# Centred input in pieces, second half one step later, and another order at the start

## Chip, core and metric

The kernel runs on one core of one Trainium2 chip. The metric is the device time of one execution in microseconds. Engines: TensorE (PE), VectorE (DVE), ScalarE (ACT), GpSimd (POOL) and SyncE (SP), which issues the transfers.

## What is computed

`x` is 4 sequences of 1024 tokens with 128 features. Four layers, each on a layer norm of x and added to it:

```
x = x + attn_a(ln(x))    # inside: conv of 4 taps, q/k/v with running means, a small gelu FFN
x = x + ffn(ln(x))       # sum over 8 experts: (silu(x Wg) * (x Wu)) Wd, 128 -> 512 -> 128
x = x + attn_b(ln(x))    # 16 heads of 8, ALiBi, causal
x = x + ffn(ln(x))       # the same experts again
```

`attn_a` on one sequence h = ln(ln(x)): `x1 = ln(x) + conv(h)`, then `q, k, v` of ln(x1); `pq = cumsum(q) / position`, `pk = cumsum(pq * k) / position`, `x2 = x1 + pk * v`, and `x2 + Wu gelu(Wb ln(x2))`. Only the first layer (the "sequence work") and the first FFN are touched here.

## The kernel before

**Tiles.** A sequence is 8 blocks of 128 tokens (`BLK`), in two halves of 512 (u = 0, 1). The FFN goes over 8 tiles of 512 tokens; a tile has 32 chunks of 128 hidden features. x lies in SBUF all the time.

**The first FFN with the sequences beside it.** `ffn(f)` runs pairs of tiles (= one sequence). In a pair there are 64 steps p, one per chunk. In step p TensorE does the sequence stages of p, then gate and up of chunk p + 2 (L1118 to L1120, twice three products), then down of chunk p (L1125 to L1127). ScalarE does silu of chunk p + 1 (L1639), the rounded part `h_hi` of chunk p (L1657), then its sequence stages. VectorE does the product of chunk p + 1 (L2093), the rest `h_lo` of chunk p (L2114), then its stages. The down product of p waits for `h_hi` and `h_lo` of p. Each engine takes its stream in order. The first pair is written out ("first"), the next two are a loop ("middle"), the last has no sequence beside it. Pair i has sequence i + 1 beside it.

**The order of the sequence work** is a table by hand, `AT`: for each stage the step for half 0 and for half 1. `at(p, kind)` asks whether a stage is due at p: in the first pair ten steps later than the table (`SHIFT_FIRST`), in the middle pairs three later (`TAPS_LATER`) for all but `tok`, `T1` and `copy`. Stages in the order of data: `tok` centres the input by blocks, four per half, on VectorE (`a0_tok`, L1926) and on ScalarE (`hc_tok`, L1542); `T1` transposes both; `copy` takes them from PSUM; `conv` (L879 in the middle pairs, from `taps`, which SyncE writes to memory and loads back shifted, L583 and L586); `a1` (L1935) adds; `T5`, `stats5` (L1903, L1907), `norm5` (L1553), `T7`, `h2`; `q`, `cumq`, `k`, `kq`, `cumk`, `v`, `vq`; `T9`, `stats9`, `norm9` (L1553), `T10`, `h3` (L1560); `up` (L943; four products; for half 1 all in one step, with the four copies `hid1` on VectorE, L1988, one step earlier in the table); `gelu` (L1573, all four parts at once, with a load of ScalarE's gelu table before it and one of silu's after it); `down` (L952), `y` (L1992), `T13`, `x1` (L1996). GpSimd has the roots of the inner norms, the two means (L677, L680) and one addition (L684). The norm of the next tile stands at `NORM_AT`: in middle pairs statistics at step 10, norm (L1874) at 13, transposes at 14.

```
       "up": (32, 37), "gelu": (36, 41), "down": (42, 44), "y": (43, 45), "T13": (44, 46),
UP_AT = [AT["up"][0] + c for c in range(4)] + [AT["up"][1]] * 4
    return UP_AT[4] - 1 if name == "hid1" else AT[name][u]
```

So in a middle pair the gelu of half 0 is at step 39, the up products of half 1 at step 40 and the gelu of half 1 at step 44, with the down products of half 0 at step 45.

**The start.** Sequence 0 runs before the FFN, half 0 ahead; the order is written out by calls `first_step(stage, u)` in every engine. VectorE's `stats_of_input(lo, hi)` takes statistics of input blocks (L1894, L1897). GpSimd's `low_part(r, m)` (L689) splits a quarter of a weight; `norms_of_input` takes the roots for all blocks and waits for all statistics. Stages that half 1 of sequence 0 has left run in the first steps of the first pair (`LEFT`, `left(p)`).

Of the kernel before, what the change touches and what calls it, by code (L numbers as in the profile page):

```python
# [140 lines left out]
def rests_by_pool(p):  # L141
# [9 lines left out]

AT = {"tok": (0, 1), "T1": (2, 4), "copy": (2, 4), "conv": (5, 6), "a1": (6, 7), "T5": (7, 8),
# [11 lines left out]
SHIFT_FIRST = 10  # L166
NORM_AT = {"first": (12, 24), "middle": (10, 16), "last": (13, None)}
LOW_LATE = 13
LEFT = {"stats9": 0, "norm9": 2, "T10": 3, "h3": 3, "up": (4, 4, 5, 5), "hid1": (4, 4, 5, 5), "gelu": 6,
        "down": (8, 8, 9, 9), "y": 9, "T13": 10, "x1": 10}  # L170


def position(name, u, c=0):

    if name in ("up", "down"):
        return (UP_AT if name == "up" else DOWN_AT)[u * 4 + c]
    return UP_AT[4] - 1 if name == "hid1" else AT[name][u]


# [3 lines left out]
def at(p, kind):  # L183

    def now(name, u, c=0):
        later = 0
        if kind == "first":
            later = SHIFT_FIRST
        elif name not in AHEAD_OF_TAPS:
            later = TAPS_LATER  # L190
        return position(name, u, c) + later == p
    return now

# [19 lines left out]
def only(*wanted):  # L213
    return lambda *stage: stage == wanted
# [14 lines left out]
def build(nc, ap):  # L229
    x_in, out = ap["hidden"], ap["out"]  # L230
    with ExitStack() as ctx:
# [366 lines left out]
        def _(pool):  # L598
# [105 lines left out]
            pool.wait_ge(s["a_n5"], BLK)  # L704
            low_part(1, 1)
            low_part(1, 2)
            low_part(2, 0)
            low_part(2, 1)
            pool.wait_ge(s["rinv_ready"], 5)
            sequence_step(0, only("cumq", 1), True)  # L710
            sequence_step(0, only("cumk", 1), True)

            def rstd4(f, n0, mv=mv, lnw=lnw):
# [41 lines left out]
            def ffn_beside_sequences(f):  # L755

                def norm(t):
                    pool.wait_ge(f["mv"], t * SUB + SUB)
                    rstd4(f, t * 2)

                def pair(i, kind):
                    for p in range(2 * CH):
                        if kind == "first" and p == LOW_LATE:
                            pool.wait_ge(s["a_tokd"], 2 * BLK)
                            for m in range(3):
                                low_part(3, m)
                        sequence_step(i + 1, at(p, kind))
                        if p % CH == NORM_AT[kind][p // CH]:
                            norm(i * 2 + (p // CH + 1))

                norm(0)
                pool.wait_ge(f["norm"], SUB)
                low_part(2, 2)
                sequence_step(0, left(0), True)
                norms_of_input(BLK, B * BLK)
                pair(0, "first")
                with pool.Fori(1, TILES // 2 - 1) as i:
                    pair(i, "middle")
                for p in range(2 * CH):
                    if p == NORM_AT["last"][0]:  # L780
                        norm(TILES - 1)
                    if p >= PROJECT_FROM and (p - PROJECT_FROM) % PROJECT_STEPS == 2:
                        root_of_projected((p - PROJECT_FROM) // PROJECT_STEPS)
                    if p in REST_BY_POOL:
                        pool.wait_ge(f["hhi"], LAST_PAIR + p + 1)
                        g.tensor_tensor(h_lo[:, p % 2, :], hid[:, p % 4, :], h_hi[:, p % 2, :].bitcast(F32),
                                        ALU.subtract).then_inc(f["hlo_pool"], 1)
                    if p >= PROJECT_FROM:
                        project_step(*divmod(p - PROJECT_FROM, PROJECT_STEPS))
                    if p == SPLIT_EARLY:  # L790
                        split_max(0)
                third_part(LAST - 1, 1)
# [52 lines left out]
        def _(pe):  # L845
# [115 lines left out]
            def first_step(*stage):  # L961
                sequence_step(0, only(*stage), True)
# [40 lines left out]
            first_step("T5", 1)  # L1003
            first_step("T10", 0)
            first_step("T7", 1)
            for c in range(4):
                first_step("up", 0, c)
            first_step("q", 1)
            first_step("k", 1)
            for c in range(4):  # L1010
                first_step("down", 0, c)
# [482 lines left out]
        def _(act):  # L1494
# [32 lines left out]
            def sequence_step(b, now, first=False):  # L1527

                for u in range(2):
                    ahead = first and u == 0  # L1530
                    src, sl = bank(0 if ahead else 5 + u), slice(u * NT, (u + 1) * NT)
                    blocks = range(SUB * u, SUB * (u + 1))
                    if now("tok", u):

                        if first:
                            act.wait_ge(s["a_lnx"], 9 * (u + 1))
                        else:
                            act.wait_ge(s["a_lns"], b)
                            act.wait_ge(s["a_dn"], b * 2)
                        ln = lnx if first else lns  # L1540
                        for j in blocks:
                            a.activation(hc_tok[:, j * P:(j + 1) * P], xs(b * BLK + j), ACT.Identity,  # L1542
                                         bias=ln[:, L_BOTH_BIAS, j:j + 1],
                                         scale=ln[:, L_BOTH, j:j + 1]).then_inc(s["a_toka"], 1)
# [31 lines left out]
            def first_step(*stage):  # L1576
                sequence_step(0, only(*stage), True)
# [4 lines left out]
                for m in range(3):  # L1582
                    a.copy(w_hi[m][:, quarter], w_raw[m][:, quarter]).then_inc(s[f"split_hi{r}"], 1)

            first_step("tok", 0)
            conv_matrices()
            act.wait_ge(s["par_ready"], 1)
            first_step("copy", 0)
            high_part(0)
            first_step("tok", 1)  # L1590
            other_matrices()
            first_step("copy", 1)
            first_step("h2", 0)
# [242 lines left out]
        def _(dve):  # L1836
# [71 lines left out]

            def sequence_step(b, now, first=False):

                if now("tok", 0) and not first:

                    v.tensor_copy(lns[:], lnx[:, :, bass.ds(b * BLK, BLK)]).then_inc(s["a_lns"], 1)
                    dve.wait_ge(s["a_lns"], b)
                for u in range(2):
# [1 line left out]
                    src, other = (bank(0), bank(1)) if ahead else (bank(5 + u), bank(6 - u))  # L1917
                    sl = slice(u * NT, (u + 1) * NT)
                    blocks = range(SUB * u, SUB * (u + 1))
                    if now("tok", u):  # L1920
                        if first:
                            dve.wait_ge(s["a_lnx"], 9 * u + 2)
                        for j in blocks:
                            mean = mvx[:, j, 0:1] if first else lns[:, L_MEAN, j:j + 1]
                            rstd = (lnx if first else lns)[:, L_RSTD, j:j + 1]
                            v.tensor_scalar(a0_tok[:, j * P:(j + 1) * P], xs(b * BLK + j), mean, rstd,  # L1926
# [77 lines left out]
                stats_of_input(u * SUB, u * SUB + SUB)  # L2004
            positions()
            quarter_of_positions(0)
            first_step("tok", 0)
            quarter_of_positions(1)
            parameters()
            first_step("copy", 0)  # L2010
            first_step("tok", 1)
            quarter_of_positions(2)
            dve.wait_ge(s["par_ready"], 1)
            first_step("a1", 0)
# [16 lines left out]
            projections()  # L2031
            v.memset(x[:, 0:NT], 0.0)
            dve.wait_ge(s["x_rest_loaded"], 16 * (B - 1))
            stats_of_input(BLK, 2 * BLK + SUB)
            first_step("cumq", 1)
            first_step("kq", 1)
            first_step("cumk", 1)
            first_step("y", 0)
# [50 lines left out]
            def ffn(f):  # L2089
# [9 lines left out]
                def pair(i, kind):  # L2099
                    last = kind == "last"  # L2100
                    for h in range(2):
                        t = i * 2 + h
                        end = last and h == 1
                        for c in range(CH):
# [18 lines left out]
                                continue  # L2123
                            if kind == "first":
                                sequence_step(0, left(h * CH + c), True)
                            if kind == "first" and h * CH + c == SHIFT_FIRST:
                                dve.wait_ge(s["a_lnx"], 28)
                            if not last:
# [12 lines left out]
                                project_step(*divmod(c - PROJECT_FROM, PROJECT_STEPS))  # L2141

                first_norm(f, 5)
                stats_of_input(2 * BLK + SUB, B * BLK)
                dve.wait_ge(f["up"], 1)
                dve.wait_ge(f["silu"], 1)
                product(0)
# [276 lines left out]
```

## Time and profile before

| | us |
|---|---|
| median of 3 runs | 1780.88 (1780.56 to 1783.27) |
| profiled execution | 1783.65 |
| its span, first to last instruction | 1781.9 |
| mean granted TensorE clock | 0.986 |
| first FFN, first to last gate/up product | about 61 to 765 |

In a row of the timeline stand: start in us from the span's start, length in us, engine, line, operation, output <- inputs, shapes, count of merged instructions, and in brackets the engine's idle time just before and what ended it. A product of 512 columns follows the one before it after 0.23 us at the full clock.

### The profile page before, as it was taken

Reading aid. Unit: us, or ns where it says so; the run is one execution under the profiler, and the core shown is the slowest. Engines: PE = TensorE matmul, PEld = TensorE weight load, DVE = VectorE, ACT = ScalarE, POOL = GpSimd, SP = SyncE. Lnnn points to the kernel's source line nnn. Section 1 sums busy time; section 2 is a strip of 40 time slices with the busy share of each in tenths; the row PEclk is TensorE's granted clock in tenths of the full one; section 3 lists DMA queues with packets and bytes.
Section 4 is the critical chain, followed back from the end, with each engine's and each line's share of the span. In section 5 each row is a group of like instructions: output and inputs, shape, how many; then the busy total and the mean of one; then the engine's idle time right before and its main releaser. Section 6 shows DMA issues by size and latency. Waiting matters only on the chain.

```text
span 1781.9 us, 28475 instructions
## 1 busy us (share of the span) xinstructions
PE 1694.8 (95%) x10265; PEld 1098.4 (62%) x10265; DVE 1256.3 (71%) x2133; ACT 1039.4 (58%) x1690; POOL 478.2 (27%) x648
## 2 busy tenths in 40 slices
PE   5799999999999999988889999999999999999998
PEld 3567677777767877633335555555555555558876
DVE  7677577766766777777777777777777777646665
ACT  6445755555565555466656666566666566665554
POOL 6522001100210123421114444334444443440000
PEclk8899999999999999989999999999999999999999
DMA  6000011002000122223010100000000000010000
GB/s 213 0 1 1 1 30 31 1 1 59 4 0 0 41 88 84 84 78 101 28 46 2 36 24 20 7 24 25 14 24 24 18 8 2 2 31 1 6 7 6
DMA packets 63423, 52.35 MB, mean 29 GB/s; under 512 B 7983, under 2 KB 58558, under 8 KB 63294
## 3 DMA queue, kind: packets, MB, share of 16 engines
q1 hardware_dynamic: 63120, 50.57, 9.7%
q8 instruction: 79, 1.29, 0.3%
q14 instruction: 50, 0.41, 0.1%
q10 hardware_dynamic: 174, 0.07, 0.0%
HBM read 32.40 MB, written 18.22 MB: 28 GB/s over the span
## 4 chain that ended last, share of the span: by engine, by line
PE 81%; DVE 7%; ACT 5%; issue 3%; DMA 1%; POOL 1%; SPq 0%; ACTq 0%; DVEq 0%
PE ps L1263 8%; PE ps L1226 7%; PE ps L1264 6%; PE ps L1265 6%; PE ps L1118 5%; PE ps L1120 5%; PE ps L1119 5%; PE ps L1091 4%; PE ps L1295 4%; PE ps L1060 3%; PE ps L849 3%; PE ps L1297 3%; PE ps L1296 3%; PE ps L1125 3%; PE ps L1127 3%
## 5 line engine op out<-in xcount | busy, mean ns | idle before, releaser
L1633 ACT ACTIVATE pr<-ps 128x1024 f32<-128x1024 f32 (+2 forms) x285 | 267.8, 945 | 188.7 <-PE ps L1048 115.5
L2093 DVE TENSOR_TENSOR hid<-sg,ps 128x512 f32<-128x512 f32 x256 | 174.8, 683 | 192.2 <-PE ps L1120 142.4
L809 POOL TENSOR_TENSOR h_lo<-hid,h_hi 128x512 fp32r<-128x512 f32 x176 | 225.6, 1282 | 265.2 <-ACT h_hi L1733 260.7
L1639 ACT ACTIVATE sg<-ps 128x512 f32<-128x512 f32 x256 | 153.7, 600 | 238.1 <-PE ps L1120 235.7
L2083 DVE TENSOR_REDUCE negp<-ps 128x2 f32<-128x1024 f32 (+2 forms) x224 | 254.6, 1145 | 51.0 <-PE ps L1048 30.4
L1118 PE MATMUL ps<-xn_hi,w_hi 128*128 128x512 f32 x512 | 227.3, 444 | 0.6 <-DVE xn_lo L1889 0.6
L1263 PE MATMUL ps<-xn_hi,w_hi 128*128 128x512 f32 x512 | 223.5, 437 | 0.7 <-DVE hid L2220 0.6
L2220 DVE SCALAR_TENSOR_TENSOR hid<-sg,ps 128x512 f32<-128x512 f32 x176 | 121.0, 687 | 126.4 <-ACT sg L1723 125.7
L1264 PE MATMUL ps<-xn_lo,w_hi 128*128 128x512 f32 x512 | 202.2, 395 | 0.0
L1120 PE MATMUL ps<-xn_hi,w_lo 128*128 128x512 f32 x512 | 202.1, 395 | 0.0
L1119 PE MATMUL ps<-xn_lo,w_hi 128*128 128x512 f32 x512 | 202.0, 394 | 0.0
L1265 PE MATMUL ps<-xn_hi,w_lo 128*128 128x512 f32 x512 | 201.4, 393 | 0.0
L2114 DVE TENSOR_TENSOR h_lo<-hid,h_hi 128x512 fp32r<-128x512 f32 x236 | 176.0, 746 | 0.0
L1733 ACT CAST h_hi<-hid 128x512 fp32r<-128x512 f32 x256 | 157.5, 615 | 14.6 <-PE ps L1297 10.2
L1657 ACT CAST h_hi<-hid 128x512 fp32r<-128x512 f32 x256 | 157.6, 616 | 0.6 <-DVE hid L2093 0.4
L1723 ACT ACTIVATE sg<-ps 128x512 f32<-128x512 f32 x176 | 105.4, 599 | 77.3 <-PE ps L1265 76.0
L1226 PE MATMUL ps<-pr,vp 128*9 128x512 f32 (+3 forms) x1376 | 146.2, 498 | 0.0
L1091 PEld LDWEIGHTS ps<-qs,ks 63*128 63x128 bf16 x720 | 35.1, 93 | 168.0 <-issue 141.5
L1091 PE MATMUL ps<-qs,ks 63*128 63x512 bf16 (+2 forms) x720 | 114.5, 335 | 13.8 <-DVE negp L2083 9.7
L2226 DVE TENSOR_TENSOR hid<-hid,ps 128x512 f32<-128x512 f32 x176 | 120.3, 684 | 7.1 <-PE ps L1265 3.1
L1263 PEld LDWEIGHTS ps<-xn_hi,w_hi 128*128 128x128 f32 x512 | 95.9, 187 | 40.4 <-issue 18.7
L1060 PE MATMUL ps<-ks,qs 60*128 60x512 bf16 (+2 forms) x720 | 113.1, 330 | 6.2 <-DVE xn_lo L2210 2.6
(244 smaller groups left out, 3074.5 us busy)
## 6 DMA issues: line engine op xcount, KB each, us to landing
qs<-qd SPq DMA_DIRECT2D x60, 96.0 KB
ks<-kd SPq DMA_DIRECT2D x60, 96.0 KB
kd<-qkp SPq DMA_DIRECT2D x14, 256.0 KB, 2.9
qd<-qkp SPq DMA_DIRECT2D x7, 384.0 KB, 2.6
w_raw<-in_Wg SPq DMA_DIRECT2D x4, 512.0 KB, 7.4
w_raw<-in_Wu SPq DMA_DIRECT2D x4, 512.0 KB, 7.4
w_raw<-in_Wd SPq DMA_DIRECT2D x4, 512.0 KB, 8.7
work<-hd SPq DMA_DIRECT2D x8, 256.0 KB, 4.5
```

The costliest lines, as they stand in the source:

```text
L809: g.tensor_tensor(h_lo[:, q % 2, :], hid[:, q % 4, :], h_hi[:, q % 2, :].bitcast(F32), ALU.subtract).then_inc(FS[1]["hlo_pool"], 1)
L1091: mm = pe.matmul(dst[e], k_of(n)[r, hp, j * P:(j + 1) * P], q_of(n)[r, hp, from_q:from_q + w], start=True, stop=st not in MASKED)
L1118: pe.matmul(dst, w_hi[m][:, w], xn_hi[:, h, :], start=True, stop=False)
L1119: pe.matmul(dst, w_hi[m][:, w], xn_lo[:, h, :], start=False, stop=False)
L1120: pe.matmul(dst, w_lo[m][:, w], xn_hi[:, h, :], start=False, stop=True).then_inc(f[sig], 1)
L1226: mm = pe.matmul(ps[32 * h:32 * h + HD + 1, O_BANK, from_q:NT], vp[:, n % 2, j, h, :], pr_of(n, st)[:, h, 0:NT - from_q], start=(j == 0), ...
L1263: pe.matmul(dst, w_hi[m][:, w], xn_hi[:, h, :], start=True, stop=False)
L1264: pe.matmul(dst, w_hi[m][:, w], xn_lo[:, h, :], start=False, stop=False)
L1265: pe.matmul(dst, w_lo[m][:, w], xn_hi[:, h, :], start=False, stop=True).then_inc(f[sig], 1)
L1633: a.activation(pr_of(n, st)[:].rearrange("p (e a) q -> p e a q", e=2)[:, :, hps[0]:hps[-1] + 1, 0:WIDTH[st]], heads(buf, hps, WIDTH[st]), ...
L2083: v.tensor_reduce(to[:, :, hps[0]:hps[-1] + 1, i % SUB], heads(buf, hps, JOB_WIDTH[k]), AX.X, ALU.max, negate=True).then_inc(T["reduced"], 1)
L2114: v.tensor_tensor(h_lo[:, c % 2, :], hid[:, c % 4, :], h_hi[:, c % 2, :].bitcast(F32), ALU.subtract).then_inc(f["hlo"], 1)
```

## The change

It centres the input of a sequence in two pieces per half, two blocks each, at table steps 0, 1 (half 0) and 2, 3 (half 1), on both engines. In the middle pairs every other stage of half 1 but `T1` and `copy` comes one step later. In the start, TensorE does `q` of half 1 after two of the four up products of half 0; VectorE takes only four blocks of statistics near there (behind `cumq`), twelve at the FFN's start, and eight in pieces of two in steps 0 to 3; GpSimd does `cumq` after the low parts of quarter 1, one low part between the two means, one before the stages left over and one behind the first of them.

```diff
-AT = {"tok": (0, 1), "T1": (2, 4), "copy": (2, 4), "conv": (5, 6), "a1": (6, 7), "T5": (7, 8),
+AT = {"T1": (2, 4), "copy": (2, 4), "conv": (5, 6), "a1": (6, 7), "T5": (7, 8),
+TOK_AT = ((0, 1), (2, 3))
+    if name == "tok":
+        return TOK_AT[u][c]
@@ at
         elif name not in AHEAD_OF_TAPS:
-            later = TAPS_LATER
+            later = TAPS_LATER + u
@@ GpSimd, start
             low_part(1, 2)
-            low_part(2, 0)
-            low_part(2, 1)
             pool.wait_ge(s["rinv_ready"], 5)
             sequence_step(0, only("cumq", 1), True)
+            low_part(2, 0)
             sequence_step(0, only("cumk", 1), True)
@@ GpSimd, before the first pair
                 pool.wait_ge(f["norm"], SUB)
+                low_part(2, 1)
+                sequence_step(0, left(0), True)
                 low_part(2, 2)
-                sequence_step(0, left(0), True)
                 norms_of_input(BLK, B * BLK)
@@ TensorE, start
-            for c in range(4):
-                first_step("up", 0, c)
+            first_step("up", 0, 0)
+            first_step("up", 0, 1)
             first_step("q", 1)
+            first_step("up", 0, 2)
+            first_step("up", 0, 3)
             first_step("k", 1)
@@ ScalarE and VectorE, sequence_step
-                    if now("tok", u):
+                    for c in range(2):
+                        if not now("tok", u, c):
+                            continue
...
-                        for j in blocks:
+                        for j in blocks[2 * c:2 * c + 2]:
@@ VectorE, start
-            stats_of_input(BLK, 2 * BLK + SUB)
+            dve.wait_ge(s["rinv_ready"], 5)
             first_step("cumq", 1)
+            stats_of_input(BLK, BLK + SUB)
             first_step("kq", 1)
@@ VectorE, pair
                                 sequence_step(0, left(h * CH + c), True)
+                            if kind == "first" and h == 0 and c < SUB:
+                                stats_of_input(3 * BLK + 2 * c, 3 * BLK + 2 * c + 2)
...
-                stats_of_input(2 * BLK + SUB, B * BLK)
+                stats_of_input(BLK + SUB, 3 * BLK)
```

## Rows read from the trace of the kernel before

**Rows 1.** The page, busy time and share of each engine.
```profile
PE 1694.8 (95%) x10265; PEld 1098.4 (62%) x10265; DVE 1256.3 (71%) x2133; ACT 1039.4 (58%) x1690; POOL 478.2 (27%) x648
```

**Rows 2.** Timeline of TensorE, two successive down products, second middle pair.
```profile
538.84 0.40 PE L1125 MATMUL ps<-h_hi,w_hi 128*128 128x512 f32 x1
...
540.91 0.40 PE L1125 MATMUL ps<-h_hi,w_hi 128*128 128x512 f32 x1
```

**Rows 3.** Timelines of the start, VectorE and TensorE; last a window, PEclk the third from its end.
```profile
42.04 2.35 DVE L1894 BATCH_NORM_STATS2 stx<-x 128x6 f32<-128x128 f32 x12
...
50.01 0.75 DVE L1961 SCALAR_TENSOR_TENSOR work<-ps,par,work 128x512 f32<-128x512 f32 x1 [2.91 <-POOL work L677]
...
52.00 0.73 DVE L1992 SCALAR_TENSOR_TENSOR a0T<-ps,par,a0T 128x512 f32<-128x512 f32 x1
...
46.48 3.60 PE L952 MATMUL ps<-gel_first,wt 128*128 128x512 f32 x8
...
60.00:65.00 5.00, 4.36 (x12) 3.18 (x11) 4.50 (x26) 2.09 (x3) 0.85 (x1) 0.50 0.00 0
```

**Rows 4.** Timelines of GpSimd and VectorE, first pair, step 14.
```profile
111.12 7.93 POOL L689 TENSOR_TENSOR w_lo<-w_raw,w_hi 128x1024 fp32r<-128x1024 f32 x3
...
111.46 2.60 DVE L2114 TENSOR_TENSOR h_lo<-hid,h_hi 128x512 fp32r<-128x512 f32 x1
```

**Rows 5.** Timelines of ScalarE and TensorE, second middle pair, steps 0 and 1.
```profile
423.31 1.65 ACT L1542 ACTIVATE work<-x,lns 128x128 f32 x4 [1.81 <-DVE lns L1913]
...
426.98 0.47 PE L1125 MATMUL ps<-h_hi,w_hi 128*128 128x512 f32 x1 [1.42 <-DVE h_lo L2114]
```

**Rows 6.** Timelines of TensorE and VectorE, second middle pair, steps 9 to 13.
```profile
446.80 0.64 PE L879 MATMUL ps<-taps,w_taps 128*32 128x512 f32 x4 [0.91 <-DMA taps<-hd]
...
450.70 0.74 DVE L1935 SCALAR_TENSOR_TENSOR a0T<-ps,par,a0T 128x512 f32<-128x512 f32 x1
...
456.12 0.88 DVE L1903 BATCH_NORM_STATS2 sta<-ps 128x6 f32<-128x128 f32 x4
...
458.51 1.11 DVE L1874 TENSOR_SCALAR ntok<-x,mv,lnw 128x128 f32 x4
```

**Rows 7.** Timelines of ScalarE and TensorE, second middle pair, steps 33 and 34.
```profile
510.00 1.54 ACT L1553 ACTIVATE work<-ps,lna 128x128 f32<-128x128 f32 x4
...
510.50 0.47 PE L1125 MATMUL ps<-h_hi,w_hi 128*128 128x512 f32 x1
...
513.57 0.47 PE L1125 MATMUL ps<-h_hi,w_hi 128*128 128x512 f32 x1
```

**Rows 8.** Timelines of ScalarE, TensorE and VectorE, second middle pair, steps 39 and 40.
```profile
526.48 1.28 ACT L1573 ACT_TABLE_LOAD   x1
...
529.70 1.28 ACT L1639 ACT_TABLE_LOAD   x1
531.00 0.60 ACT L1639 ACTIVATE sg<-ps 128x512 f32<-128x512 f32 x1
531.49 0.61 ACT L1657 CAST h_hi<-hid 128x512 fp32r<-128x512 f32 x1
...
528.63 3.85 PE L943 MATMUL ps<-h2T,wt 128*128 128x512 f32 x8
...
534.62 0.47 PE L1125 MATMUL ps<-h_hi,w_hi 128*128 128x512 f32 x1 [0.74 <-ACT h_hi L1657]
...
529.70 1.61 DVE L1988 TENSOR_SCALAR work<-ps,par 128x512 f32<-128x512 f32 x2 [2.35 <-PE ps L943]
...
533.79 0.69 DVE L2114 TENSOR_TENSOR h_lo<-hid,h_hi 128x512 fp32r<-128x512 f32 x1
```

**Rows 9.** TensorE, first pair, steps 7 and 8: timeline, and the windows' row behind the gap.
```profile
90.39 0.76 PE L1125 MATMUL ps<-h_hi,w_hi 128*128 128x512 f32 x1 [2.94 <-ACT h_hi L1657]
...
95.83 0.40 PE L1125 MATMUL ps<-h_hi,w_hi 128*128 128x512 f32 x1
...
90.22:93.63 3.41, 3.23 (x6) 1.94 (x7) 1.23 (x3) 0.14 (x1) 0.00 (x0) 0.50 0.02 5
```

More of the change, by code:

```diff
@@ L1583, in high_part @@
                     a.copy(w_hi[m][:, quarter], w_raw[m][:, quarter]).then_inc(s[f"split_hi{r}"], 1)
-            first_step("tok", 0)
+            for c in range(2):
+                first_step("tok", 0, c)
             conv_matrices()
@@ L1589, in _ @@
             high_part(0)
-            first_step("tok", 1)
+            for c in range(2):
+                first_step("tok", 1, c)
             other_matrices()
@@ L1909, in sequence_step @@
             def sequence_step(b, now, first=False):
-                if now("tok", 0) and not first:
+                if now("tok", 0, 0) and not first:
                     v.tensor_copy(lns[:], lnx[:, :, bass.ds(b * BLK, BLK)]).then_inc(s["a_lns"], 1)
@@ L1919, in sequence_step @@
                     blocks = range(SUB * u, SUB * (u + 1))
-                    if now("tok", u):
+                    for c in range(2):
+                        if not now("tok", u, c):
+                            continue
                         if first:
                             dve.wait_ge(s["a_lnx"], 9 * u + 2)
-                        for j in blocks:
+                        for j in blocks[2 * c:2 * c + 2]:
                             mean = mvx[:, j, 0:1] if first else lns[:, L_MEAN, j:j + 1]
@@ L2006, in _ @@
             quarter_of_positions(0)
-            first_step("tok", 0)
+            for c in range(2):
+                first_step("tok", 0, c)
             quarter_of_positions(1)
@@ L2010, in _ @@
             first_step("copy", 0)
-            first_step("tok", 1)
+            for c in range(2):
+                first_step("tok", 1, c)
             quarter_of_positions(2)
```

## The prediction

> **What bounds the kernel now.** I read the page first: TensorE is busy for 95% of the span [rows 1], and no other engine is near that. So a microsecond counts only where TensorE stands still or runs at its lower clock. Then I read TensorE's timeline in the first FFN (63 to 765 us), the only part the change touches besides the start. Its unit is the step: the interval between the starts of two successive down products. A step that carries nothing of the sequence work takes 2.07 us [rows 2]; four transposes add 0.43 and a sequence product of 512 columns 0.87. What an interval has beyond such a sum is a stall. In the middle pairs (two passes of the loop, steps 0 to 63 each, the same pattern in both) I find these, each the distance of two down products less their work: step 0, 1.36 and 1.68 us; the tap transfers before the second convolution, about 1.2; steps 12 to 14, 0.9 in all; steps 25 to 28, 1.2; steps 32 and 33, 0.9; the gelu of the first half, 1.14.
>
> **The start.** VectorE does twelve statistics blocks before the scan of q, GpSimd is in its low parts and multiplies the mean only behind them, and the product with k waits 2.91 us for that mean, until 50.01 [rows 3]. The residual at L1992 comes at 52.00, though its four down products ended at 50.08 [rows 3]. After the change, q comes two products earlier on TensorE, only four blocks stand beside it, and GpSimd is free after two low parts. The total of TensorE's work up to the down products is the same. So L1992 is released by them: 50.15, a gain of 1.85, carried by the transpose, the addition, the statistics and the norm to the first gate product.
>
> Part of it goes back. Four steps now each carry two blocks of statistics on VectorE, about 0.65 us (0.4 for the blocks at the rate of the twelve at 42.04 [rows 3], the rest for two aggregates and their wait). In step 1 VectorE is the late one, because it has just done the inner statistics: 0.65 us of stall. The last low part of quarter 2 also moves behind the inner statistics of GpSimd, beside `h_lo`. What that does stands in the trace: with low parts running from 111.12, an `h_lo` of usually 0.69 takes 2.60 [rows 4]. VectorE and GpSimd take turns; one pass of about 2.6 (7.93 over three) delays the `h_lo` of step 2 by about 0.9 more. The Trainium skill (GPSIMD Engine Reference, Key points) speaks of contention with VectorE instructions that have two SBUF inputs; that speaks against this move, and the trace agrees, 2.60 against 0.69. Together the give-back is 1.5. Against it, TensorE's first gate and up products run at the half clock (0.50 from 60 to 65, its lower level of 1.2 GHz [rows 3]). They start 1.85 us earlier; if the clock also rises earlier by more than that, some of the products at 0.43 become 0.23. I take **-1.2** for the start, between -0.3 (clock rises when it did) and -2.0 (it rises before the first product).
>
> **The input in pieces.** At step 0 ScalarE has four activations of 1.65 us in one step and then silu and cast; TensorE stands 1.42 us before the next down product [rows 5]. Half of the activations leave 0.8 us less in front of the silu. The other halves move to steps 1, 2 and 3, where ScalarE has 0.8 us left over in a step of 2.07. The copy of the per-block constants, for which they wait, stays. So **-0.85** per middle pass and **-0.45** in the first pair, where the low parts of quarter 3 wait for the last piece, start 0.3 us later and meet the `h_lo` that TensorE waits for.
>
> **Second half one step later, steps 8 to 14.** The second convolution sits 0.91 us waiting for its taps after a half-empty slot [rows 6]. One step later the taps have been in for over 1 us: -1.15. But now step 11 on VectorE holds first the inner statistics of half 0 (1.3) and then the addition a1 of half 1 (0.74 [rows 6]), on which TensorE's transposes wait at the start of step 12: stall 0.66. And step 13 holds the inner statistics of half 1 (1.3, from 456.12) and the norm of the next tile (1.11 [rows 6]) together, so the transposes of that tile wait 1.15 instead of 0.3. Worked through to step 14 it is **+0.2** per pass: what the taps give, VectorE takes. Its ends are -1.2 (VectorE catches up) and +1.0 (GpSimd's passes fall on it too).
>
> **Steps 22 to 30.** The scan of q moves behind the product with v in the same step and TensorE's v product waits 0.6; one of the stalls behind GpSimd's passes at steps 26 to 28 goes. **+0.2** per pass, from -0.5 to +1.0.
>
> **Steps 32 to 35.** ScalarE now does h3 of half 0 and then the norm of half 1 (1.54) in one step, and the step takes 3.07 [rows 7], 0.57 more than its work. Apart, neither is late: **-0.6** per pass.
>
> **The gelu of half 0, the largest term.** It stays at step 39, since it belongs to half 0: table load, 1.91 us, table load, 526.48 to 530.98, and ScalarE's silu and cast of step 40 come behind it, the cast ending at 532.10 [rows 8]. Today TensorE fills that time with the four up products of half 1, which stand at step 40: 528.63, 3.85 us long [rows 8]. They belong to half 1 and move to step 41. Step 40 then has only a gate/up pair: TensorE is through with it at 530.02 and waits for `h_lo` of step 40, which can start at 532.1 and takes 0.69 [rows 8], so the down product starts at 532.98. That is a **gap of 2.96 us**. Then come the up products, with VectorE's four copies (from 529.70 today) between them. Today the down product stands 4.92 behind the first of those copies (534.62 [rows 8]); tomorrow the first copy is at 534.75, so the down product of step 41 is at 539.67. Today it is at 536.77: **+2.9** per pass. The gelu of half 1 moves with its half to step 45, where the down products of half 0 still stand; ScalarE starts it about 2 us later than today's, is done at 548.0, and TensorE has work until 550.6. Zero.
>
> Here a rule competes with the trace. From the rows, the silu starts 0.02 us behind its table load of 1.28, and I used that. The Trainium skill (ScalarE: Activation LUTs, What ACT_TABLE_LOAD costs) gives 2.66 us for every switch of tables with its drain. By that the gap would be 2.8 us longer per pass and my sum 5.5 higher.
>
> **The clock.** The trace has one other gap of this length in this part: 2.94 us before 90.39, also behind a gelu. The granted clock is 0.50 (1.2 GHz) for the 3.4 us behind it, and the interval to 95.83 is 5.44 us instead of 3.80 [rows 9]: 1.64 lost. Each of the two new gaps can cost between 0 (the clock stays, as behind the 1.42 of [rows 5]) and 1.6. I take 1.5, since they are nearest to the gap of 2.94.
>
> **Sum.** Start -1.2, first pair -0.45, per middle pass -0.85 + 0.2 + 0.2 - 0.6 + 2.9 + 1.5 = 3.35, twice 6.7: **+5.05**. The profiled execution took 1783.65, so 1788.7 for such a one; it lies 2.8 above the median of the runs shown, so I forecast a median of 1785.9. A measurement here can tell about 0.2% (3.6 us) from nothing.
>
> **Rivals.**
> - *The gap is there, but the clock stays up, and the small terms fall on the good side* (start -1.6, steps 8 to 14 at 0): -1.6 - 0.45 + 2 x 1.65 = +1.25, 1782.1: no change. For it: behind the 1.42 us of [rows 5] the clock stayed at 1.00. Against: 2.94 did. 0.30.
> - *The gelu stays covered and nothing new is late* (the other side). Place: the down product of step 40. If TensorE has as much queued before it as today, the penalties of steps 12 to 14, 22 to 30 and 40 vanish: -1.2 - 0.45 - 2 x (0.85 + 1.15 + 0.6) = -6.85, 1774.0. It decides from where the penalties of a pass stay under 1.65 us together; I have nearly 6. Against it: ScalarE runs in order, and nothing of step 40 can pass the table loads. 0.13.
> - *The rule of the tables holds where TensorE waits for ScalarE*, a drain of 1.38 per load that only shows then: 1785.9 + 5.5 = 1791.4. Against: the cast behind the loads is timed. 0.05.
> - My forecast: 0.52.
>
> **The numbers.** Slower by over 0.2% has the forecast and the table rival, 0.57; within 0.2%, 0.30; faster, 0.13. The low end, 1777.5, has the lower bounds of the terms (start -2.0, steps 8 to 14 at -1.2, no clock) and leaves most of the covered case out; the high end, 1790.5, has the clock at 1.6 twice and both VectorE terms at their upper bounds.
>
> **What would show it.** Right: in both middle passes a TensorE gap of nearly 3 us before the down product of step 40, behind an ACT cast, and 0.50 of clock behind it; no wait for taps; the second norm at step 34 without a stall; the transposes of step 12 waiting for a1, those of step 14 for the norm; L1992 near 50.1; one `h_lo` over 1.5 us near 71. Wrong: no gap at step 40, or up products still in front of it; taps still awaited; a start that is not earlier at the first gate product.

## The result, and the profile after

The changed kernel takes 1794.57 us, the median of six runs; the kernel before, run beside it, takes 1782.08. The ratio is 1.0064, its 95% interval 1.0052 to 1.0075: 11.4 us slower, between 9.3 and 13.4 (the two medians lie 12.5 apart). The forecast was slower by 5.05, with 1790.5 as the high end. The sign was right; the size was not.

The profiled execution has a span of 1794.6 against 1781.9, 12.7 more. The starts of the down products cut the first FFN into pairs and steps, and that shows where the 12.7 us arise.

| us | before | after | change |
|---|---|---|---|
| start of the second pair, from the span's start | 253.07 | 253.79 | +0.71 |
| first middle pass, 64 steps | 170.16 | 175.39 | +5.23 |
| second middle pass | 169.71 | 174.53 | +4.82 |
| last pair | 171.30 | 171.26 | -0.04 |
| from the FFN's last down product to the end | 1017.68 | 1019.60 | +1.92 |

And within the middle passes, the first and the second of them. A step p is here the time from the start of its down product to that of the next one:

| steps | before | after | change | forecast |
|---|---|---|---|---|
| 0 to 3, the pieces | 11.95, 12.28 | 11.55, 11.88 | -0.40, -0.40 | -0.85 |
| 7 to 14 | 22.42, 22.65 | 22.86, 22.85 | +0.44, +0.20 | +0.2 |
| 20 to 29 | 25.61, 25.59 | 26.65, 26.68 | +1.04, +1.09 | +0.2 |
| 31 to 35 | 14.37, 14.38 | 13.82, 13.81 | -0.55, -0.57 | -0.6 |
| 39 and 40, the gelu, with the clock | 8.84, 8.83 | 13.41, 13.48 | +4.57, +4.65 | +4.4 |

**The gelu of the first half.** TensorE's timeline in the first middle pass, as in [rows 8]: the down product of step 40, the up products of half 1, the down product of step 41.

```profile
363.71 0.48 PE L1130 MATMUL ps<-h_hi,w_hi 128*128 128x512 f32 x1 [2.97 <-ACT h_hi L1665]
...
364.49 5.29 PE L946 MATMUL ps<-h2T,wt 128*128 128x512 f32 x8
...
371.91 0.47 PE L1130 MATMUL ps<-h_hi,w_hi 128*128 128x512 f32 x1 [0.75 <-ACT h_hi L1665]
```

ScalarE's timeline in the same place: the two table loads, the silu and the cast. VectorE's `h_lo` of step 40, the last line, starts behind the cast and ends at 363.56; the down product waits for both, and starts 0.15 us behind it. (Its row names the cast, which had ended at 362.67.)

```profile
357.05 1.28 ACT L1579 ACT_TABLE_LOAD   x1
358.34 1.92 ACT L1579 ACTIVATE work<-work 128x2048 f32<-128x2048 f32 x1
360.28 1.28 ACT L1647 ACT_TABLE_LOAD   x1
361.57 0.60 ACT L1647 ACTIVATE sg<-ps 128x512 f32<-128x512 f32 x1
362.06 0.61 ACT L1665 CAST h_hi<-hid 128x512 fp32r<-128x512 f32 x1
...
362.88 0.68 DVE L2127 TENSOR_TENSOR h_lo<-hid,h_hi 128x512 fp32r<-128x512 f32 x1
```

The gap is 2.97 us, and behind it the four up products (eight matmuls) take 5.29 us where they took 3.85 [rows 8]. Windows in the gap, right behind it, and further on (PEclk is the third column from the end):

```profile
361.50:365.00 3.50, 1.29 (x5) 0.95 (x6) 1.29 (x2) 2.17 (x5) 0.00 (x0) 1.00 0.00 0
365.08:368.49 3.41, 3.41 (x5) 1.13 (x5) 1.50 (x2) 0.00 (x0) 0.00 (x0) 0.50 0.00 0
368.60:372.00 3.40, 2.65 (x10) 1.45 (x9) 2.94 (x5) 1.22 (x2) 0.00 (x0) 1.00 0.00 0
```

The clock is at its lower level of 1.2 GHz for 3.41 us, as behind the gap of [rows 9]; the second pass shows the same (0.50 from 539.16 to 542.57).

**The start.** TensorE from the transposes of T7 to the transposes that wait for L2002 (L1992 in the kernel before):

```profile
39.87 1.12 PE L852 MATMUL ps<-ident,work 128*128 128x128 f32 x4 [0.25 <-DVE work L1953]
...
47.65 3.60 PE L955 MATMUL ps<-gel_first,wt 128*128 128x512 f32 x8
51.08 1.02 PE L920 MATMUL ps<-h2T,wt 128*128 128x512 f32 x2
52.23 0.66 PE L852 MATMUL ps<-ident,a0T 128*128 128x128 f32 x4
```

And the same stretch before, whose row of the down products is in [rows 3]:

```profile
39.31 1.12 PE L849 MATMUL ps<-ident,work 128*128 128x128 f32 x4 [0.25 <-DVE work L1943]
...
49.91 1.02 PE L917 MATMUL ps<-h2T,wt 128*128 128x512 f32 x2
52.78 0.66 PE L849 MATMUL ps<-ident,a0T 128*128 128x128 f32 x4 [1.85 <-DVE a0T L1992]
```

The wait of 1.85 us that was to go is gone: TensorE now works through. But the down products end at 51.25 (50.08 before [rows 3]), and the last transposes start at 52.23, only 0.55 earlier. The stretch begins 0.56 later (39.87 against 39.31), and its product with v comes 1.17 later (51.08 against 49.91), so 0.61 more was lost on the way. That is in the clock, as the windows of before and after show (PEclk 0.76 and 0.58): counted from the stretch's own start, about 3.1 us at half clock before and 4.3 after, which costs 0.6 us more. Why the stretch begins later stays open.

```profile
40.00:45.00 5.00, 5.00 (x12) 2.38 (x11) 4.91 (x26) 4.16 (x6) 5.00 (x3) 0.76 0.01 3
```

```profile
40.00:45.00 5.00, 5.00 (x10) 2.53 (x11) 2.62 (x5) 3.76 (x5) 4.62 (x2) 0.58 0.01 3
```

**The give-back.** VectorE's timeline at the end of the start, then the `h_lo` of step 2 of the first pair:

```profile
48.24 0.75 DVE L1971 SCALAR_TENSOR_TENSOR work<-ps,par,work 128x512 f32<-128x512 f32 x1 [0.34 <-POOL work L680]
49.03 2.50 DVE L1978 TENSOR_TENSOR_SCAN work<-work,zcol 128x512 f32<-128x512 f32 x1
...
70.99 2.20 DVE L2127 TENSOR_TENSOR h_lo<-hid,h_hi 128x512 fp32r<-128x512 f32 x1
```

GpSimd beside them, the low part between the two means and the one behind the stages left over:

```profile
48.10 2.34 POOL L692 TENSOR_TENSOR w_lo<-w_raw,w_hi 128x1024 fp32r<-128x1024 f32 x1
...
70.25 2.40 POOL L692 TENSOR_TENSOR w_lo<-w_raw,w_hi 128x1024 fp32r<-128x1024 f32 x1
```

The product with k, which waits for the mean of q, waits 0.34 where it waited 2.91 [rows 3]. The `h_lo` takes 2.20 us beside GpSimd's low part. TensorE's down products of steps 1 and 2 then wait 0.76 (at 69.97) and 1.04 us (at 73.34). Steps 0 and 1 take 3.09 and 3.37 us where they took 2.44 and 2.17: +1.85.

**Steps 7 to 14.** TensorE's convolution, the transposes of step 12 and those of step 14:

```profile
278.18 1.07 PE L882 MATMUL ps<-taps,w_taps 128*32 128x512 f32 x8
...
284.07 0.65 PE L852 MATMUL ps<-ident,a0T 128*128 128x128 f32 x4 [0.47 <-DVE a0T L1945]
...
289.71 0.66 PE L852 MATMUL ps<-ident,ntok 128*128 128x128 f32 x4 [0.82 <-DVE ntok L1882]
```

**Steps 22 to 30.** TensorE's product with v and two later down products:

```profile
316.40 1.12 PE L920 MATMUL ps<-h2T,wt 128*128 128x512 f32 x2 [0.46 <-DVE work L1961]
...
326.89 0.48 PE L1130 MATMUL ps<-h_hi,w_hi 128*128 128x512 f32 x1 [0.45 <-ACT h_hi L1665]
...
332.02 0.47 PE L1130 MATMUL ps<-h_hi,w_hi 128*128 128x512 f32 x1 [0.73 <-DVE h_lo L2127]
```

GpSimd and VectorE ahead of the last of them: the addition on GpSimd, and the `h_lo` beside it, which is twice as long as usual (0.68).

```profile
330.03 1.29 POOL L687 TENSOR_TENSOR a0T<-a0T,work 128x512 f32<-128x512 f32 x1 [0.93 <-DVE work L1987]
```

```profile
330.47 1.41 DVE L2127 TENSOR_TENSOR h_lo<-hid,h_hi 128x512 fp32r<-128x512 f32 x1
```

In the kernel before, the same addition stood 4 us earlier, beside another `h_lo`, and TensorE waited 0.36 us for that one (GpSimd, VectorE, TensorE):

```profile
326.15 1.29 POOL L684 TENSOR_TENSOR a0T<-a0T,work 128x512 f32<-128x512 f32 x1
...
326.49 1.50 DVE L2114 TENSOR_TENSOR h_lo<-hid,h_hi 128x512 fp32r<-128x512 f32 x1
...
328.13 0.47 PE L1125 MATMUL ps<-h_hi,w_hi 128*128 128x512 f32 x1 [0.36 <-DVE h_lo L2114]
```

### The profile page after: what moved, and what is told of

It is laid out like the page before. It is cut to its first block, busy times and chain, and to the rows that moved or that the text cites. A ratio compares the mean times of both kernels' runs of the same rounds, so it can differ in the third digit from the quotient of the medians.

```text
span 1794.6 us, 28482 instructions
## 1 busy us (share of the span) xinstructions
PE 1700.7 (95%) x10265; PEld 1101.4 (61%) x10265; DVE 1257.7 (70%) x2133; ACT 1039.4 (58%) x1690; POOL 483.5 (27%) x648
## 4 chain that ended last, share of the span: by engine, by line
PE 79%; DVE 9%; ACT 5%; issue 4%; POOL 2%; SPq 0%; DMA 0%; ACTq 0%; DVEq 0%; POOLq 0%
PE ps L1268 8%; PE ps L1231 7%; PE ps L1269 6%; PE ps L1270 6%; PE ps L1123 5%; PE ps L1125 5%; PE ps L1124 5%; PE ps L1096 4%; PE ps L1300 4%; PE ps L1065 3%; PE ps L852 3%; PE ps L1302 3%; PE ps L1301 3%; PE ps L1130 3%; PE ps L1132 3%
## 5 line engine op out<-in xcount | busy, mean ns | idle before, releaser
L1741 ACT CAST h_hi<-hid 128x512 fp32r<-128x512 f32 x256 | 157.5, 615 | 14.6 <-PE ps L1302 10.2
L1130 PE MATMUL ps<-h_hi,w_hi 128*128 128x512 f32 x256 | 104.8, 409 | 21.9 <-ACT h_hi L1665 12.8
```

## The experiments

Each kernel was timed in five rounds beside the kernel before; ratios are to the runs of before made beside it, with the 95% interval, and a difference in us with a sign (+7.3) is worked out from the ratio. The kernel before itself had medians of 1782.08 to 1783.74 in these groups of runs, so a comparison with the changed kernel's median of 1794.57 is rough by a microsecond or two. Edits start from the changed kernel unless another is named. "Old start" is the start of the kernel before.

**1. The gelu of half 0 moves with the up products that cover it.** All of the change stays, and the gelu of half 0 comes one step later.

```diff
-            later = TAPS_LATER + u
+            later = TAPS_LATER + (1 if u or name == "gelu" else 0)
```

> The changed kernel, with one thing more: in the middle pairs the gelu of half 0 also comes one step later (step 40), again one step in front of the up products of half 1. Theory A (the loss is the gelu that lost its cover, and the clock that falls behind the gap): no TensorE gap near 3 us at step 40, no half clock there, 4.5 us less per pass, so 9 us below the changed kernel and about 3 above the kernel before. Theory B (the loss lies with VectorE and GpSimd in steps 8 to 30 and the gap only takes waits that would come anyway): at most 3 us below the changed kernel.

Measured: 1785.17, ratio 1.0009 [1.0000, 1.0018], 9.4 us under the changed kernel's median. Steps 39 and 40 are back to 8.76 us in both passes, and the up products stand in front of the down product again:

```profile
531.11 3.85 PE L946 MATMUL ps<-h2T,wt 128*128 128x512 f32 x8
```

So most of the loss hangs on the place of the gelu against the up products.

**2. Nothing but the up products late**, in the kernel before.

```diff
-            later = TAPS_LATER
+            later = TAPS_LATER + (1 if u and name in ("up", "hid1") else 0)
```

> The kernel before, with only the four up products of half 1 and their copies (hid1) one step later in the middle pairs. Theory A: the same gap of 2.96 us before the down product of step 40 in both passes, 0.50 of clock behind it, steps 39 and 40 together 13.4 instead of 8.8 us, so 9 us above the kernel before; 6 if the clock does not fall. Theory B: under 3 us above.

Measured: 1791.37, ratio 1.0041 [1.0027, 1.0054], +7.3 us. TensorE's timeline shows the gap without anything else of the change:

```profile
360.57 0.48 PE L1125 MATMUL ps<-h_hi,w_hi 128*128 128x512 f32 x1 [2.96 <-ACT h_hi L1657]
...
361.35 5.29 PE L943 MATMUL ps<-h2T,wt 128*128 128x512 f32 x8
```

Steps 39 and 40 take 13.40 and 13.62 us. The two passes are 4.87 and 4.42 us longer than before, 9.3 together, and the part behind the FFN happens to be 2.2 shorter in this profile. By the measured time this one move costs about two thirds of the whole loss.

**3, 4 and 5. The three parts alone.** Start only (TOK_AT as before, no shift), pieces only (old start, no shift), shift only (in the kernel before).

```diff
# start only
-TOK_AT = ((0, 1), (2, 3))
+TOK_AT = ((0, 0), (1, 1))
-            later = TAPS_LATER + u
+            later = TAPS_LATER
# shift only, in the kernel before
-            later = TAPS_LATER
+            later = TAPS_LATER + u
```

> The changed kernel without the shift of half 1 and with both pieces of a half in one step as before: only the start is in the new order. My prediction: 1.2 us below the kernel before. Rival, from the changed kernel's trace (a gain of 1.8 up to the first gate product, and 1.85 given back in steps 0 and 1): no difference, between -0.5 and +1.

Measured: 1785.75, ratio 1.0007 [0.9998, 1.0016], +1.3 us. The forecast's -1.2 fails: the interval reaches from -0.4 to +2.9.

> The kernel before, with only the centred input in pieces. My prediction: -0.45 in the first pair and -0.85 in each middle pass, 2.2 us below the kernel before. Rival, from the changed kernel's trace (0.77 less at step 0, 0.32 more at step 2): about -0.45 a pass, 1.3 below in all.

Measured: 1781.17, ratio 0.9991 [0.9981, 1.0002], -1.6 us, which could still be nothing; the forecast's -2.2 and the rival's -1.3 both lie in the interval. Steps 0 to 3 take 11.55 and 11.87, as in the changed kernel.

> The kernel before, with only the shift of half 1 by one step in the middle pairs. My prediction's terms for it (+0.2, +0.2, -0.6, +2.9 and 1.5 of clock, twice) give 8.4 us above the kernel before. Rival, from the traces so far (4.56 a pass at steps 39 and 40, and nearly +1.0 instead of +0.2 at steps 20 to 30): 10.5 to 11.5 above, if the clock falls in both passes.

Measured: 1788.91, ratio 1.0048 [1.0034, 1.0062], +8.6 us. In the first pass steps 39 and 40 take 13.61, in the second 11.96. The gap is there in the second pass too (TensorE's timeline), but this time the clock stays at its full level behind it (window):

```profile
537.30 0.48 PE L1125 MATMUL ps<-h_hi,w_hi 128*128 128x512 f32 x1 [2.96 <-ACT h_hi L1657]
```

```profile
537.30:540.70 3.40, 3.40 (x9) 1.51 (x9) 1.45 (x2) 0.00 (x0) 0.00 (x0) 1.00 0.00 0
```

That separates the two terms: 11.96 - 8.84 = 3.12 us for the gap, and 1.45 to 1.65 for the clock where it falls.

**6. The start without its give-back.** Both low parts of quarter 2 ahead of the stages left over, the eight late statistics blocks in steps 2 to 5; no pieces, no shift.

```diff
                 low_part(2, 1)
+                low_part(2, 2)
                 sequence_step(0, left(0), True)
-                low_part(2, 2)
-                            if kind == "first" and h == 0 and c < SUB:
-                                stats_of_input(3 * BLK + 2 * c, 3 * BLK + 2 * c + 2)
+                            if kind == "first" and h == 0 and 2 <= c < 2 + SUB:
+                                stats_of_input(3 * BLK + 2 * c - 4, 3 * BLK + 2 * c - 2)
```

> The start in the new order alone (as in e3_start_only), but GpSimd's last low part of quarter 2 directly behind the one before it, in its idle time before the inner statistics, and the eight late statistics blocks in steps 2 to 5 instead of 0 to 3. If the give-back in steps 0 and 1 is this low part beside h_lo and the statistics on a late VectorE: no h_lo over 1 us and no stall near step 1, 1.8 us below e3_start_only, about 0.5 below the kernel before. If it is something else (the T10 or the norm of half 1): no difference from e3_start_only.

Measured: 1782.48, ratio 1.0005 [0.9994, 1.0017]. Steps 0 and 1 are back to 2.44 and 2.15, and the `h_lo` of step 2 is short:

```profile
70.68 0.68 DVE L2127 TENSOR_TENSOR h_lo<-hid,h_hi 128x512 fp32r<-128x512 f32 x1
```

The give-back is shown in the profile; the edit moves the low part and the statistics together, so it doesn't separate the two. In the time it is too small to be seen: 1.0005 and 1.0007 of experiment 3 have overlapping intervals.

The profiles of all the kernels say more of the start than the one pair does: the mean clock from 40 to 45, the start of the transposes that wait for L2002 (or L1992), and of the first down product.

| start | profiles | clock, 40 to 45 | transposes | their wait | first down product |
|---|---|---|---|---|---|
| old | 5 | 0.57 to 0.76, mean 0.64 | 52.78 to 53.33, mean 53.10 | 1.20 to 1.85 | 67.22 to 68.17, mean 67.65 |
| new | 9 | 0.50 to 0.80, mean 0.62 | 51.21 to 53.84, mean 52.11 | none shown | 65.34 to 68.37, mean 66.68 |

The wait is gone in all nine. What comes of it is 1.0 us at the transposes and 1.0 at the first down product, and it scatters more: over 2.6 us at the transposes, where the old start has 0.54. This fits a wait that absorbed a slow clock in the old start and is missing in the new one; no run tests it by itself.

**7. Only the moves that gained.** Experiment 6's start and the pieces; of half 1, only the convolution and the stages norm9, T10 and h3 come later.

```diff
-            later = TAPS_LATER + u
+            later = TAPS_LATER + (1 if u and name in ("conv", "norm9", "T10", "h3") else 0)
```

> Pieces, the start of e6_low_part_early, and of half 1 only the convolution and norm9, T10 and h3 one step later in the middle pairs; all else of half 1 stays. If the taps' 1.15 us a pass are to be had when a1 and stats5 stay where they are: no taps wait, steps 8 to 14 at -1 a pass, -0.55 a pass at steps 33 and 34, 5.5 us below the kernel before. If VectorE takes the taps' gain back here too: 3.2 below.

Measured: 1777.83, ratio 0.9975 [0.9965, 0.9986]: 4.5 us faster than the kernel before (between 2.5 and 6.2), and some 16 under the changed kernel. The interval holds both of the expected times; the profile decides between them: steps 7 to 14 fall to 21.44 and 21.43. TensorE's convolution and the next tile's transposes wait for nobody:

```profile
276.29 1.07 PE L882 MATMUL ps<-taps,w_taps 128*32 128x512 f32 x8
...
286.41 0.66 PE L852 MATMUL ps<-ident,ntok 128*128 128x128 f32 x4
```

**8. The whole chain up to h2 late.** As 7, with a1, T5, stats5, norm5, T7 and h2 of half 1 late as well.

```diff
+            ("conv", "a1", "T5", "stats5", "norm5", "T7", "h2", "norm9", "T10", "h3")
```

> As e7_conv_and_norm9_late, but all stages of half 1 from the convolution to h2 one step later; q to stats9 and the gelu's neighbours stay. If steps 8 to 14 of the change are lost to VectorE (the second inner statistics and the norm in one step): +0.3 to +0.5 there a pass, and 2 to 3 us above e7_conv_and_norm9_late. If not: the same as it. In both, steps 20 to 30 as in the kernel before if the q to stats9 shift made that loss.

Measured: 1781.23, ratio 0.9989 [0.9980, 0.9998]. Steps 7 to 14 are at 22.87 and 22.86, and both waits of the changed kernel are back:

```profile
284.71 0.66 PE L852 MATMUL ps<-ident,a0T 128*128 128x128 f32 x4 [0.47 <-DVE a0T L1945]
...
290.37 0.66 PE L852 MATMUL ps<-ident,ntok 128*128 128x128 f32 x4 [0.83 <-DVE ntok L1882]
```

The intervals of experiments 7 and 8 overlap a little; in the profiles the two middle passes take 335.6 and 338.3 us together (339.9 in the kernel before). So the convolution's delay is worth about 1.1 us a pass, and delaying the rest of its chain takes 1.4 back. Steps 20 to 29 are at 25.60, as before: their +1.04 comes from the stages behind h2.

**9. The gap filled with products that nobody reads.** The changed kernel, with 11 extra gate products ahead of the down product of step 40.

```diff
+if kind == "middle" and p == UP_AT[3] + TAPS_LATER + 2:
+    pe.wait_ge(s["a_hid0"], (i + 1) * 4 + 4)
+    for _ in range(11):
+        pe.matmul(bank(5), w_hi[0][:, 0:P], xn_hi[:, 1, :], start=True, stop=True)
```

> The changed kernel with eleven products without use (of 0.23 us, into the bank that the up products overwrite next) on TensorE in front of the down product of step 40 in the middle pairs; they fit in the gap of 2.97 us. If the gap itself makes the clock fall: no 0.50 near step 40, step 40 takes 6.8 instead of 8.2 us in both passes, and the kernel is 2.5 to 3 us faster than the changed one. If the clock falls for another reason: the same falls and the same time as the changed kernel.

Measured: 1791.40, ratio 1.0049 [1.0031, 1.0067], 3.4 us under the changed kernel's median beside it (1794.85, experiment 12). Their intervals overlap; the profiles show the gain where it was expected, 346.9 us for the two middle passes against 349.9. TensorE's timeline, the extra products, the down product and the up products; then the window behind them:

```profile
358.92 2.65 PE L1191 MATMUL ps<-xn_hi,w_hi 128*128 128x512 f32 x11
362.05 0.47 PE L1130 MATMUL ps<-h_hi,w_hi 128*128 128x512 f32 x1 [0.47 <-ACT h_hi L1669]
...
362.82 3.85 PE L946 MATMUL ps<-h2T,wt 128*128 128x512 f32 x8
```

```profile
365.00:368.50 3.50, 3.05 (x10) 1.43 (x8) 3.03 (x5) 1.02 (x2) 0.00 (x0) 1.00 0.00 0
```

Steps 39 and 40 take 11.96 in both passes: the path is as long as with a bare gap, 3.12 over the kernel before, and the clock does not fall. The clock's share is thus 1.5 a pass. Some bare gaps left the clock up too (the last section), so two filled ones alone would not prove that the gap lowers it. But from 100 to 760 us none of the 14 profiles has half clock anywhere except behind a bare gap of 2.96 or 2.97 us.

**10, 11 and 12. Two parts together, and the changed kernel again.** Shift and pieces with the old start; shift and start (TOK_AT = ((0, 0), (1, 1))); the changed kernel unaltered.

> The changed kernel with the start of the kernel before. The parts alone measured +8.6 (shift), -1.6 (pieces), +1.3 (start); the changed kernel +11.4, which leaves 3 us. If the parts add up and the rest is scatter of the clock: 7 above the kernel before, and 10 to 11 with the changed kernel measured again beside it not above 9.5. If the start costs more together with the shift (its late statistics and low part are 1.3 alone): 7 above here, 11.4 again for the changed kernel.

Measured: 1791.72, ratio 1.0055 [1.0035, 1.0074], +9.8 us.

> The changed kernel with both pieces of a half in one step, as before. If the parts add up: 9.9 above the kernel before, 1.6 above the changed kernel. If the pieces and the shift get in each other's way (ScalarE or VectorE late at step 8 because of the pieces): below the changed kernel.

Measured: 1792.78, ratio 1.0057 [1.0040, 1.0074], +10.2 us. The clock falls at the first gap (13.63) and not at the second (11.96).

> The changed kernel unaltered, beside the others on the same chip. If the parts add up: 8.3 above the kernel before. If not: 11.4 as measured first. Its profile shows again at which of the two gaps the clock falls: at both if the rule is one of the gap alone, at one or the other if the instant of the gap decides, as in e5_shift_only.

Measured: 1794.85, ratio 1.0064 [1.0048, 1.0080]. The clock falls at both gaps again (13.40 and 13.45), and the part behind the FFN is 1019.68, as in the first profile (1019.60).

The parts alone add up to 8.6 - 1.6 + 1.3 = +8.3 us, the whole has +11.4 [9.3, 13.4]. Given the parts' own intervals that is no contradiction, and the runs don't settle whether something joins them.

**What lies behind the FFN.** The code there is the same in all these kernels, yet its time differs by 6 us from profile to profile. I added up the time at half clock in the 240 us behind 764 us, from windows of 6 us ((1 - clock) x 12 each), in all 14 profiles. Eight of them:

| kernel | half clock, us | FFN's last down product to the end |
|---|---|---|
| experiment 7 | 13.0 | 1013.67 |
| experiment 10 | 13.7 | 1013.57 |
| experiment 2 | 20.4 | 1015.45 |
| before | 23.6 | 1017.68 |
| experiment 1 | 23.9 | 1017.15 |
| experiment 4 | 27.1 | 1018.10 |
| changed, again | 30.6 | 1019.68 |
| changed | 30.7 | 1019.60 |

The other six lie between 20.4 and 23.9 us of half clock and 1015.08 and 1017.98. One window each of the kernel before and of the changed one, where attention begins:

```profile
769.47:779.71 10.24, 7.79 (x43) 2.40 (x43) 7.53 (x15) 5.00 (x8) 2.86 (x8) 0.50 0.65 204
```

```profile
778.00:795.20 17.20, 14.47 (x82) 4.79 (x82) 10.67 (x22) 8.79 (x14) 4.78 (x9) 0.50 0.51 153
```

So the 1.92 us between these two profiles behind the FFN go with 7.1 us more at half clock. Each row is one execution, and single executions of one kernel differ by more than that: the 62 of the kernel before that were run beside the experiments take 1777.7 to 1787.5 us, on the mean 1784.2 where the mean granted clock is 0.986 and 1781.1 where it is 0.988. Experiment 7's profile is of the fastest of its eight runs (1774.16). The changed kernel's two profiles agree, 30.7 and 30.6, but of the kernel before there is only one. So it isn't shown that the 1.92 us come from the change, and what decides how long the clock stays down there is open.

## Why the prediction was right and wrong

**Right: the gelu.** The gap was forecast at 2.96 and is 2.97, behind the cast and the `h_lo` that were named. The path term was +2.9 and measures 3.12 (experiments 5, 9 and 11). The clock term was 1.5 and measures 1.45 to 1.65. Together 4.4 was forecast, 4.57 and 4.65 came. Experiments 1 and 2 show it from both sides. The rival that the clock stays up holds for single gaps (experiments 5 and 11, second pass), not for the changed kernel. The rival of a covered gelu fails: the gap is there. For the drain of the tables, the silu starts 0.01 us behind its load (360.28 + 1.28, 361.57) and the gap is 2.97, not 5.8. The Trainium skill (ScalarE: Activation LUTs, What ACT_TABLE_LOAD costs) has 2.66 us for a switch; the trace doesn't agree where TensorE waits for exactly this, and the trace decides.

**Right: steps 7 to 14 and 31 to 35.** The taps are not awaited; T5 waits 0.47 (forecast 0.66), the next tile's transposes 0.82 (forecast 1.15). The sum, +0.44 and +0.20, is at the forecast's +0.2. For norm9 -0.6 was forecast and -0.55 came: the down products around it stand at 341.62 and 343.77, 2.15 apart, not 3.07 [rows 7].

**Wrong: the start, forecast -1.2.** Two steps of it failed, and a third had no cost in it.
- "So L1992 is released by them: 50.15, a gain of 1.85" took the down products' end from one profile as fixed. They end at 51.25 and L2002 starts at 51.45. The wait is 1.20 to 1.85 over the profiles of the old start, and once it is gone TensorE's own products decide, at whatever clock they get. The transposes gain 1.0 on the mean and the first down product 1.0. Forecast up to there were 1.85 and, by the sum, 0.85 for the clock's earlier rise, 2.7 in all, since 1.5 was to go back.
- The give-back was put at 1.5 and is 1.85: 0.65 ahead of the down product of step 1, as forecast, and 1.20 ahead of that of step 2, where 0.9 was forecast for the `h_lo` beside the low part (2.20 long). Experiment 6 removes both.
- The low part between the two means was costed at nothing. It runs beside the scan for k's mean, which takes 2.50 us there instead of 1.28. The scan ends at 51.53 and L2002 comes right behind, while TensorE is at its product with v until 52.10 and goes on at 52.23, so here it costs 0.13 us at most.

At the first down product the changed kernel is 1.05 ahead, behind step 1 it is 0.80 behind, and with the rest of the first pair 0.71. Forecast up to there: -1.2 - 0.45 = -1.65. **That is 2.4 us of the miss.** The pieces gave about -0.45 in the first pair, as forecast: from its first down product to the next pair's it takes 186.8 to 186.9 us with them and 187.3 without, in the profiles of the new start that have a clock fall of 3.41 us there. So about 1.7 of the 2.4 are the gain that was too high, 0.35 the give-back, and some 0.4 lie in the rest of the first pair and have no named cause.

**Wrong: the pieces, forecast -0.85 a pass, -0.40 came.** "ScalarE has 0.8 us left over" in steps 1 to 3 was right for ScalarE alone. Step 0 gained 0.77. But in step 2 ScalarE first has its copy from PSUM (L1553), 1.11 us idle ahead of it, and now two blocks behind that, in front of the silu; the product and `h_lo` follow late. ScalarE's timeline, then TensorE's down products of steps 1 and 3:

```profile
258.30 0.78 ACT L1553 ACTIVATE hT<-ps,par 128x512 f32<-128x512 f32 x1 [1.11 <-PE ps L852]
258.98 0.87 ACT L1548 ACTIVATE work<-x,lns 128x128 f32 x2
259.75 0.58 ACT L1647 ACTIVATE sg<-ps 128x512 f32<-128x512 f32 x1
```

```profile
256.45 0.48 PE L1130 MATMUL ps<-h_hi,w_hi 128*128 128x512 f32 x1 [0.42 <-DVE h_lo L2127]
...
261.86 0.47 PE L1130 MATMUL ps<-h_hi,w_hi 128*128 128x512 f32 x1 [0.16 <-DVE h_lo L2127]
```

I had summed ScalarE's time in the step and not asked when its work may begin. Step 2 gives back 0.32 in the first pass (2.39 for 2.07) and 0.29 in the second. In two passes this is 0.9 of the miss.

**Wrong: steps 22 to 30, forecast +0.2, +1.04 and +1.09 came.** The wait for the scan was right (0.46, forecast 0.6). "One of the stalls behind GpSimd's passes goes" was not: GpSimd's addition a2 now falls on another `h_lo` (1.41 us long at 330.47) and TensorE waits 0.73 us there, where it waited 0.36 before. The stall moved with the stage that makes it, and grew. A third wait, 0.45 before the down product at 326.89, was not in the forecast. Experiment 8 leaves these stages where they were and has 25.60. The term lay at its upper bound of +1.0; 1.7 of the miss in two passes.

**Not in the sum: the clock behind the FFN, +1.9 in the profiles.** I held code that the change does not touch for constant. Its time goes with the half clock in it (the table above), and that varies from execution to execution. How much of it is in the measured 11.4, which is taken over all the runs and not over one pair of profiles, the runs don't settle.

Together: 2.4 + 0.9 + 1.7 + 1.9 = 6.9, and 0.4 for the gelu and 0.2 for steps 7 to 14, against 12.7 - 5.05 = 7.6 in the profiles. All these misses have one sign. Of the first four, the range's high end had let only steps 22 to 30 go up. The terms that it names, with both at their upper bounds in both passes, give 1785.9 + 3.2 + 0.2 = 1789.3 and not 1790.5, and those of the low end give 1779.3 and not 1777.5; the result lies outside either way.

## What to carry over

When half of a pipeline is moved, look for the stage of the other half that covered a long operation: here four up products of half 1 covered the table loads of half 0, and moving one without the other cost two thirds of the loss. Move by stages, not by halves: the convolution and the norm alone gained about 1.1 and 0.55 us a pass (in experiment 7, with the pieces and the start in it 4.5 us in all), where the whole half lost 8.6. And a wait behind two engines that disturb each other moves with the stage; count it as gone only if its new neighbour on the other engine is known.

## What was not expected of the hardware

- Gaps of nearly the same length are not alike to the clock. Behind 2.96 and 2.97 us it fell to 0.50 for 3.41 us in both passes of the changed kernel, twice, and in both of experiment 2, but not in the second passes of experiments 5 and 11; in the second pass of experiment 10 it stayed there for 6.83 us (steps 39 and 40 took 14.65). The gap of 2.94 before the down product of step 7 in the first pair [rows 9], from which the clock term was taken, is no different: in the profiles of experiments 2, 4 and 5 the clock stays at 1.00 there, and the time to the next down product is 3.87 us and not 5.44. What decides it is open.
- The same unchanged code behind the FFN spends from 13.0 to 30.7 us at half clock in these profiles, one execution each, and its time goes from 1013.6 to 1019.7 with it.
- A scan is held up by a GpSimd pass too: 2.50 us for 1.28, where an `h_lo` takes 2.20 for 0.68. The Trainium skill (GPSIMD Engine Reference, Key points) names VectorE instructions with two SBUF inputs; the trace agrees for `h_lo`, and the scan, which also takes a column of zeros from SBUF, fits it.
